# GpSimd's gathers of the experts' rows, four blocks at a time and each four behind its own last store

## The reference

```python
scores, idx = jax.lax.top_k(probs, K)            # 2 of 8 experts for each token
full = relu(xn @ W1_e + b1_e) @ W2_e + b2_e      # each expert e
c = jnp.einsum('ef,efh->eh', relu(b1), W2) + b2
output = jnp.sum(scores[..., None] * (sel_full - c_sel + c.sum(axis=0)), axis=2)
x = _layernorm(x + (residual + output))
```

## Time and profile before

| | before |
|---|---|
| three timed runs | 768.43, 769.62, 770.09 us, median 769.62 |
| the profiled execution's own time | 769.5 us |
| its span in the trace | 767.7 us |
| busy: PE, DVE, ACT, POOL | 704.7, 476.0, 332.5, 261.5 us |

### The profile page before, as it was taken

One profiled execution on the slowest core, in us unless ns is written; L12 is line 12 of the kernel. 1 busy time (PEld: TensorE's weight loads), 2 busy tenths in 40 slices (PEclk: granted clock), 3 DMA queues, 4 the chain that ended last, 5 costly groups with the idle time before them and its releaser, 6 DMA issues.

```text
span 767.7 us, 15240 instructions
## 1 busy us (share of the span) xinstructions
PE 704.7 (92%) x5152; PEld 615.4 (80%) x5153; DVE 476.0 (62%) x1095; ACT 332.5 (43%) x994; POOL 261.5 (34%) x215
## 2 busy tenths in 40 slices
PE   7798999999999999998989989999999999997980
PEld 6788887879889798896869978888888888786750
DVE  3635536677858767787779745555555555453476
ACT  5575776666776767677433012222122222121112
POOL 1300010121405032050733555276069300438664
PEclk9899999999999999998867999999999999998965
DMA  9467594731110020101422244245134411113124
GB/s 311 104 227 246 180 303 157 225 106 42 33 52 29 16 69 3 42 28 43 165 75 91 76 151 152 69 156 165 34 123 132 141 41 40 63 38 100 52 70 157
DMA packets 68497, 82.68 MB, mean 108 GB/s; under 512 B 5932, under 2 KB 59736, under 8 KB 68440
## 3 DMA queue, kind: packets, MB, share of 16 engines
q1 hardware_dynamic: 59800, 52.54, 21.3%
q0 software_dynamic: 8640, 29.38, 11.7%
HBM read 45.04 MB, written 36.86 MB: 107 GB/s over the span
## 4 chain that ended last, share of the span: by engine, by line
PE 77%; DVE 6%; ACT 6%; POOL 5%; issue 3%; DMA 1%; POOLq 0%; SPq 0%; ACTq 0%; DVEq 0%
PE bank L1004 15%; PE bank L752 8%; PE bank L754 7%; PE bank L753 7%; PE bank L974 5%; PE bank L976 5%; PE bank L975 5%; PE bank L984 4%; PE bank L872 4%; PE bank L931 4%; PE bank L911 3%; PE bank L923 3%; ACT arena L1104 3%; POOL arena L721 2%; PE bank L960 1%
## 5 line engine op out<-in xcount | busy, mean ns | idle before, releaser
L1004 PE MATMUL bank<-w_ring,hidT_hi 128*128 x320 | 122.0, 414 | 6.1 <-issue 5.0
L1223 ACT ACTIVATE hidT_hi<-bank 128x512 fp32r<-128x512 f32 x80 | 43.5, 596 | 181.1 <-PE bank L984 171.5
L1104 ACT ACTIVATE arena<-bank,negmx 128x128 f32<-128x128 f32 x256 | 90.8, 377 | 6.8 <-DVE negmx L1258 6.8
L1004 PE MATMUL bank<-w_ring,hidT_lo 128*128 x320 | 84.4, 284 | 0.0
L1636 DVE TENSOR_REDUCE work<-bank 128x256 f32<-128x512 f32 x40 | 27.7, 691 | 86.0 <-PE bank L1004 74.6
L1630 DVE TENSOR_TENSOR arena<-bank,b_rep 128x512 f32<-128x512 f32 x80 | 55.3, 691 | 41.0 <-PE bank L976 39.7
L1004 PEld LDWEIGHTS bank<-w_ring,hidT_hi 128*128 128x128 f32 x320 | 61.2, 191 | 18.2 <-issue 6.8
L974 PE MATMUL bank<-w_ring,xgT_hi 128*128 x160 | 66.9, 418 | 4.5 <-DVE xgT_lo L1649 2.8
L626 POOL TENSOR_TENSOR rsq<-ssq,neghalf 128x8 f32<-128x8 f32 x8 | 13.2, 1646 | 158.0 <-DVE ssq L1360 157.8
L1004 PEld LDWEIGHTS bank<-w_ring,hidT_lo 128*128 128x128 f32 x320 | 61.8, 193 | 1.9
L976 PE MATMUL bank<-w_ring,xgT_lo 128*128 x160 | 62.9, 393 | 0.0
(11 more groups left out here) (253 smaller groups left out, 1898.8 us busy)
## 6 DMA issues: line engine op xcount, KB each, us to landing
xg_dram<-zeros SPq DMA_DIRECT2D x9, 2176.0 KB, 8.6
w_raw<-in_L_ffn_W_dram POOLq DMA_DIRECT2D x16, 1024.0 KB, 6.6
y_dram<-zeros SPq DMA_DIRECT2D x2, 2560.0 KB, 10.7
work<-xg_dram SPq DMA_DIRECT2D x40, 128.0 KB, 2.1
y_dram<-work SPq DMA_DIRECT2D x40, 128.0 KB, 1.7
b_rep<-in_L_ffn_b_dram POOLq DMA_DIRECT2D x8, 512.0 KB
work<-gmax_dram SPq DMA_DIRECT2D x14, 256.0 KB, 3.6
arena<-in_x_dram SPq DMA_DIRECT2D x8, 256.0 KB, 2.7
```

Of the source, the lines that this page charges most:

```text
L1004: last = pe.matmul(o, l, r, start=c == 0 and l is both[0], stop=c == FC - 1 and l is both[0])
L1104: last = nc.scalar.activation(probs[:, n % 2, h * S:(h + 1) * S], ps_score[:, h * S:(h + 1) * S], ACT.Exp, bias=negmx[:, n % 2, h:h + 1], ...
```

## The change

- POOL waits before each four blocks, for the low rows and again for the high rows, eight times in all (`rows_stored(q, k)`). Each time it reads four limits from `stored_by` and waits on the four semaphores. The limit is the tile that holds the last row of expert 6 (low) or 7 (high) among the blocks up to that quad. With these inputs it is tile 32 for the low rows of every quad, and the tiles 33, 34, 35 and 35 for the high rows of quads 0 to 3.
- The wait for all 40 tiles now stands behind the last high gather and behind all four `rstd_of`.
- The gather of the zero rows moves from ahead of the low gathers to ahead of the high ones.
- DVE takes the additions of blocks 3, 7, 11 and 15 in place of 0 to 5, and POOL those of the other twelve (24 instructions, before 20).
- In DVE's last stage the high rows of a block (`add_high`) are now added four blocks ahead of its constants, and the first four of them ahead of the constants' chain (L1739, L1740 of the new file). `normalise_out(q - 1)` stands behind the statistics of quad q.
- The counts up to each quad come from one more small matmul on PE and wider DVE operations (320 elements where there were 40) behind the routing.

```diff
@@ -227,7 +229,7 @@
         row_f = sb("row_f", [P, 2, B])
         y_row = sb("y_row", [P, 2, B], U32)
         share, part_of = (sb(name, [P, 2, B]) for name in ("share", "part_of"))
-        stored_by = sb("stored_by", [P, DEPTH], I32)
+        stored_by = sb("stored_by", [P, 2 * QUADS * DEPTH], I32)
         y_first = sb("y_first", [P, E])
         shift = sb("shift", [P, E])
         own = sb("own", [E, E])
@@ -368,7 +370,7 @@
         LOOPED = N_TILES - 12
-        BY_DVE = 6
+        BY_DVE = 3
         assert LOOPED % DEPTH == 0
         def fillers(i, s):
@@ -710,12 +712,13 @@
             pool.wait_ge(w_split, 2 * E)
             pool.dma_start(b2_sb, b2).then_inc(b2_loaded, 16)
-            for z in range(DEPTH):
-                pool.wait_ge(y_stored[z], pool.value_load(stored_by[0:1, z:z + 1], min_val=16,
-                                                          max_val=16 * (N_TILES // DEPTH + 1)))
-                pool.sem_inc(pool_seen, 1)
-            pool.indirect_dma_start(yz, None, y_dram, bass.IndirectOffsetOnAxis(ap=zslot[:, 0:1], axis=0))\
-                .then_inc(z_gathered, 16)
+            def rows_stored(q, k):
+                for z in range(DEPTH):
+                    at = (2 * q + k) * DEPTH + z
+                    pool.wait_ge(y_stored[z], pool.value_load(stored_by[0:1, at:at + 1], min_val=16,
+                                                              max_val=16 * (N_TILES // DEPTH + 1)))
+                    pool.sem_inc(pool_seen, 1)
             def gather(k, b, landed):
                 pool.indirect_dma_start(y_all[:, k, b, :], None, y_dram,
@@ -724,26 +727,30 @@
             def add_low(b):
                 low = y_all[:, 0, b, :]
-                pool.wait_ge(low_gathered[b % 4], 16 * ((b - BY_DVE) // 4 + 1))
+                pool.wait_ge(low_gathered[b % 4], 16 * (b // 4 + 1))
                 pool.tensor_tensor(low, low, share[:, 0, b:b + 1].broadcast_to([P, D]), ALU.mult).then_inc(low_weighed, 1)
-                pool.wait_ge(low_weighed, b - BY_DVE + 1)
+                pool.wait_ge(low_weighed, b - b // 4 + 1)
                 pool.tensor_tensor(low, low, xres[:, b, :], ALU.add).then_inc(low_added, 1)
             pool.wait_ge(input_doubled, 1)
             for b in range(B):
-                gather(0, b, first_gathered if b < BY_DVE else low_gathered[b % 4])
-                if b >= BY_DVE + 2:
+                if b % 4 == 0:
+                    rows_stored(b // 4, 0)
+                gather(0, b, low_gathered[b % 4])
+                if b >= 2 and (b - 2) % 4 != BY_DVE:
                     add_low(b - 2)
-            for b in range(B - 2, B):
-                add_low(b)
+            add_low(B - 2)
+            for b in range(B):
+                if b % 4 == 0:
+                    rows_stored(b // 4, 1)
+                if b == 0:
+                    pool.indirect_dma_start(yz, None, y_dram, bass.IndirectOffsetOnAxis(ap=zslot[:, 0:1], axis=0))\
+                        .then_inc(z_gathered, 16)
+                gather(1, b, gathered[b // 2])
+            for q in range(QUADS):
+                rstd_of(q)
             for z in range(DEPTH):
                 pool.wait_ge(y_stored[z], 16 * (N_TILES // DEPTH + 1))
-            for b in range(B):
-                if b % 4 == 1 and b >= 8:
-                    rstd_of(b // 4 - 2)
-                gather(1, b, gathered[b // 2])
-            for q in range(2, QUADS):
-                rstd_of(q)
         @block.tensor
         def _(pe):
@@ -855,7 +862,9 @@
                                      chosen_sum[:, 2 * p:2 * p + 2, :].rearrange("p b e -> p (b e)"),
                                      start=False, stop=True)
                     if p == PAIRS - 1:
-                        last = pe.matmul(dst[:, 2 * E:3 * E], ones[:, :], chosen_sum[:, B, :], start=True, stop=True)
+                        pe.matmul(dst[:, 2 * E:3 * E], ones[:, :], chosen_sum[:, B, :], start=True, stop=True)
+                        last = pe.matmul(dst[:, 3 * E:3 * E + 2 * QUADS], ones[:, :], chosen_sum[:, 4:B + 1:4, E - 2:E],
+                                         start=True, stop=True)
                 last.then_inc(proj_done, 1)
             def scores(n):
@@ -1456,7 +1465,7 @@
                 un = ("R", p)
                 done(dve, un)
                 if p == PAIRS - 1:
-                    chain.link(dve.tensor_scalar(n1, ring(un)[0][:, 2 * E:3 * E], 1.0, None, ALU.add))
+                    chain.link(dve.tensor_scalar(n1, ring(un)[0][:, 2 * E:3 * E + 2 * QUADS], 1.0, None, ALU.add))
                 dve.tensor_tensor(rank, ring(un)[0][:, 0:2 * E].rearrange("p (b e) -> p b e", e=E),
                                   over_b(first_row[:, :]), ALU.add).then_inc(ring_free[place[un][0][0]], 1)
                 read(dve, un)
@@ -1570,7 +1579,7 @@
             w_cnt = wide[:, 0:E * MAX_E_TILES].rearrange("p (e j) -> p e j", e=E)
-            chain.link(dve.tensor_tensor(w_cnt, n1.unsqueeze(2).broadcast_to([P, E, MAX_E_TILES]),
+            chain.link(dve.tensor_tensor(w_cnt, n1[:, 0:E].unsqueeze(2).broadcast_to([P, E, MAX_E_TILES]),
                                          iorow[:, 0:MAX_E_TILES].unsqueeze(1).broadcast_to([P, E, MAX_E_TILES]),
                                          ALU.is_gt))
             chain.link(dve.tensor_reduce(tiles_e, w_cnt, AX.X, ALU.add))
@@ -1615,11 +1624,20 @@
                 chain.link(dve.tensor_tensor(part_of[:, :, :], score[:, :, :], part_of[:, :, :], ALU.subtract))
                 chain.link(dve.tensor_tensor(share[:, 1, :], part_of[:, 0, :], part_of[:, 1, :], ALU.add))
-                by = zeros[:, 0:N_TILES].rearrange("p (j z) -> p z j", z=DEPTH)
-                chain.link(dve.tensor_scalar(by, iotile[:, :].rearrange("p (j z) -> p z j", z=DEPTH), ends[:, E - 2:E - 1],
-                                             16.0, ALU.is_le, ALU.mult))
-                chain.link(dve.tensor_reduce(n1[:, 0:DEPTH], by, AX.X, ALU.add))
-                dve.tensor_scalar(stored_by[:, :], n1[:, 0:DEPTH], 16.0, None, ALU.add).then_inc(y_rows_ready, 1)
+                chain.link(dve.tensor_scalar(upto, n1[:, E:E + 2 * QUADS], -1.0, 1.0 / P, ALU.add, ALU.mult))
+                upto2 = upto.rearrange("p (q k) -> p q k", k=2)
+                chain.link(dve.tensor_tensor(upto2, upto2, ends[:, E - 3:E - 1].unsqueeze(1).broadcast_to([P, QUADS, 2]),
+                                             ALU.add))
+                shape = [P, 2 * QUADS, N_TILES]
+                by = wide.rearrange("p (k j) -> p k j", j=N_TILES)
+                chain.link(dve.tensor_tensor(by, iotile[:, :].unsqueeze(1).broadcast_to(shape),
+                                             upto.unsqueeze(2).broadcast_to(shape), ALU.is_le))
+                count = tile_f[:, 0:2 * QUADS * DEPTH]
+                chain.link(dve.tensor_reduce(count.rearrange("p (k z) -> p k z", z=DEPTH),
+                                             wide.rearrange("p (k j z) -> p k z j", j=N_TILES // DEPTH, z=DEPTH),
+                                             AX.X, ALU.add))
+                dve.tensor_scalar(stored_by[:, :], count, 16.0, 16.0, ALU.mult, ALU.add).then_inc(y_rows_ready, 1)
             dve.wait_ge(out_cleared, 32)
             rows_of_y()
@@ -1681,12 +1699,6 @@
                 tile(j, j % DEPTH, min(2, N_TILES - 1 - j))
-            dve.wait_ge(z_gathered, 16)
-            dve.wait_ge(b2_loaded, 16)
-            dve.tensor_tensor(dterm, yz, b2_sb, ALU.add).then_inc(c_ready, 1)
-            dve.wait_ge(csum_done, 1)
-            chain.link(dve.tensor_tensor(b2_sb, b2_sb, dterm, ALU.subtract))
-            dve.tensor_tensor(yz, b2_sb, bank[2][0:E, 0:D], ALU.add).then_inc(dterm_ready, 1)
             def constants_in(b):
                 at = (3, 4, 5, 6, 0, 1, 2, 7)[b % 8] * 512 + b // 8 * D
@@ -1703,27 +1715,37 @@
                                              rstd4[k][:, b:b + 1], ALU.subtract, ALU.mult)
                 last.then_inc(out_ready, 1)
+            def add_high(b):
+                z = y_all[:, 0, b, :]
+                dve.wait_ge(gathered[b // 2], 16 * 2)
+                if b % 4 != BY_DVE:
+                    dve.wait_ge(low_added, b - b // 4 + 1)
+                dve.scalar_tensor_tensor(z, y_all[:, 1, b, :], share[:, 1, b:b + 1], z, ALU.mult, ALU.add)\
+                    .then_inc(high_added, 1)
+            dve.wait_ge(z_gathered, 16)
+            dve.wait_ge(b2_loaded, 16)
+            dve.tensor_tensor(dterm, yz, b2_sb, ALU.add).then_inc(c_ready, 1)
             dve.wait_ge(input_doubled, 1)
-            dve.wait_ge(first_gathered, 16 * BY_DVE)
-            for b in range(BY_DVE):
+            for b in range(BY_DVE, B, 4):
+                dve.wait_ge(low_gathered[BY_DVE], 16 * (b // 4 + 1))
                 last = dve.scalar_tensor_tensor(y_all[:, 0, b, :], y_all[:, 0, b, :], share[:, 0, b:b + 1], xres[:, b, :],
                                                 ALU.mult, ALU.add)
             chain.link(last)
```

(27 more changed lines are left out.)

## The result

The changed kernel takes 772.96 us (median of five runs, 771.27 to 774.67), the kernel before 769.48 us (768.43 to 770.09) on the same chip. The ratio is 1.0049, 95% interval [1.0034, 1.0063]. The profiled execution took 771.27 us with a span of 769.5 us. The prediction was 771.7 us for it, and slower. That execution is the shortest of the five: the median lies 1.3 us above the forecast, which had put the two within 0.1 us. All medians in this text leave out three runs, one of e5 and two of c3 (the labels stand with the experiments), in which the granted clock was 0.65 and 0.82 in place of 0.95 and the time 6 to 29% longer.

The account below looks back on a forecast made before the run. POOL's high gathers and DVE were taken to set the last stage at nearly the same pace. Last `ve4` 762.8 + 5.96 + 1.1 gave a span of 769.9, so 771.7 us for the profiled execution; range 764.4 to 775.

Parts of the forecast that it names:

- The price of a set: POOL's four loads and waits before low quads 1 to 3 and high quad 0: 2.7 us each, bounds 0 to 3.6.
- Case (b): Behind an instruction that itself waits, POOL's sequencer stops, so four sets are paid: 3.56 us to the next gather, before 0.87.
- rival 1: POOL's sets are hidden everywhere, DVE alone sets the pace: 764.6 us; chance 0.17.
- POOL's course: POOL's gathers: first low at 682.9, first high at 731.0, all ended at 752.2.
- The slow gather: One gather in POOL's long run takes 2.48 us in place of 0.95; counted again, bounds 0 and 1.5.
- DVE waits for `rstd_of(0)`: At quad 1's end, `normalise_out(0)` waits for `rstd_of(0)` behind all sixteen high gathers, until 753.2; wait 1 to 2 us.
- The end: Last `ve4` at 762.8, then 5.96 us as before plus 1.1 for ACT's activations and overlapping stores.
- Rival 3: PE's 4.98 us standstill before 706.32 goes: no gain in the main case, 759.6 with hidden sets; a third of 0.17.
- the ten idle microseconds: POOL idles from the last addition at 722.90 until the last store at 733.44; the change can fill that time.

Follow-up runs that it names:

- e5: The changed kernel with the additions of blocks 0 to 6 held back behind the ninth low gather: 769.82 us, ratio to the kernel before 1.0093.
- c3: The changed kernel with one low set, high-limit loads moved early, `rstd_of(0)` behind the thirteenth high gather, constants' chain ahead of `add_high(0)`, second run: 761.28 us.
- e4: The kernel before, its high gathers waiting by four loads and waits for tiles up to the last expert's end, not all 40: 771.66 us, 1.0011.
- e9: The kernel before, high gathers released by tile 36, loads behind the second low gather, `rstd_of(0)` behind the fourteenth high gather: 767.90 us, 0.9966.
- e1: The changed kernel with one set of four loads and waits ahead of all sixteen low gathers in place of four: 766.59 us, 0.9942.
- c4: The changed kernel with one set ahead of all low gathers, run again on another chip: 766.15 us, ratio to the kernel before 0.9949.
- e3: The changed kernel with `rstd_of(0)` between the fourteenth and fifteenth high gather: 771.74 us, ratio to the kernel before 1.0024.
- e2: The changed kernel with all 32 limit loads ahead of the first wait, every wait left in place: 776.49 us, ratio to the kernel before 1.0086.

## Why the prediction was right, step by step

- **The price of a set** was 2.7 us; it measured 2.5, 2.4, 2.4 and 2.5. Case (b), that the sequencer stops at an instruction that waits, is what the traces show: of the four sets no load starts more than 0.1 us before the waiting addition does. The rule of the Trainium skill that was weighed against it ("Perfetto Trace Analysis", section "GPSIMD Engine Instruction": the sequencer is at once ready for the next instruction) would give rival 1's 764.6, and no such time came. It holds for plain gathers, under which the later loads ran.
- **POOL's course**: first low gather 682.62 (682.9 said), first high one 729.60 (731.0), the gathers' end 751.18 (752.2). It was 1.4 early: the four sets cost 1.1 us less in sum (9.7 for 10.8), and the step behind the zero rows' gather 0.25 less. The first low gather was met by luck: the wait for tile 32 ended 1.4 us earlier than said (678.5 for 679.9) and the last of the four at 680.7, but from there to the gather 1.9 us passed, where the sum has 1.0. Why is not shown. The slow gather came again.
- **DVE waits for `rstd_of(0)`** until 753.2, it said. In the profile the place is right, but what ended last there was another wait: `rstd(0)` was done at 752.25, and `ve` held until 753.36. These 1.1 us, which I hadn't foreseen, made up for the 1 us by which POOL was early. That 753.2 and then 762.8 came out so closely is luck. Without that delay (the changed kernel's second profile) the wait is for `rstd`, as said, 1.73 us.
- **The end**: 762.73 for 762.8, and 6.77 us from there to the end of the span, where 5.96 + 1.1 = 7.06 was said.
- **Rival 3, PE's stall, was read too lightly.** The text asked only what the change would gain if the stall went. It did go, and gave nothing, as said. But the other half was not asked: the ten idle microseconds which "the change can fill" were mostly the stall's own work, 7.8 of 9.8 us by the profile without it. Its price to the kernel before, 6.8 us of span, is most of what the change could win back, and it pays 9.7 us of loads and 2.6 us of further additions on POOL for it. The sign came out the same on both chips where the two were compared.

## What to carry to other kernels

A wait on a value from memory costs POOL its load, 0.57 us here, whether the semaphore is ready or not. Load behind work that the sequencer can run past (plain DMA issues), never behind an instruction that itself waits, and count how much cover there is. Finer waiting wins back only idle time that is there, and here most of it was there on some chips only: before cutting a wait, ask what makes it long, and take a profile on a second chip. When a producer moves, every hand-placed instruction between its gathers (`rstd_of(0)` here) has to be placed anew.

## What the hardware showed that was not expected

**Semaphores that arrive late, on some chips.** In all eight profiles from chips where the kernel before takes 770 us, some engine waits 1 to 6 us longer for a semaphore than its raiser's end explains. In three of them (the kernel before, e4, e9) it is in or just behind the run of nine plain low gathers, between 697 and 707; PE had then ended the tile's last matmul at 697, and DVE reduced it at 703.17. In the other five (the changed kernel, e1, c4, e3, e2) it stands at the end of the sixteen high gathers: 2.41, 2.35, 2.39, 1.06 and 1.03 us at the same `ve`, which waits for DVE's own instruction. In the six profiles from the two chips where the kernel before takes 762 us none is seen, with the same gathers. Each chip was measured on one occasion, so chip and occasion can't be told apart. Which property decides, and whether the gathers cause it, stays open: e5 was to test this, but ran where there is none.

**The slow gather.** One of the sixteen high gathers takes 2.4 to 2.9 us in place of 0.95, in every profile; none of the low ones does, not even in a run of nine. In the changed kernel and its variants it is the second high one, as in the kernel before. With the high gathers not waiting for the last store it was the ninth (e4, 2.50 us) and the sixth (e9, 2.94 us). What it is tied to wasn't tried.
